# Keeping the experts' split weights in DRAM, starting the shared tiles inside the last sequence, and a wider last matrix product

## The chip, the cores and the metric

One core of one Trainium2 chip runs one kernel. The metric is device time in microseconds, the median of the runs, lower is better. All arithmetic is float32; TensorE takes its operands as fp32r.

## The reference, cut to what matters

```python
x = x + attention(layernorm(x))      # x: (8, 256, 256), 16 heads of 128, rotary positions, causal
x = x + ffn(layernorm(x))

def ffn(hidden):                     # 2048 rows of 256, 8 experts, inner width 176, top 2
    x = hidden.reshape(-1, H)
    topk_w, topk_idx = top_k(softmax(x @ gate_w.T), 2); topk_w /= sum(topk_w)
    y_all = einsum(silu(x @ w1[e]) * (x @ w3[e]), w2[e])      # per expert e
    shared = silu(x @ sw1) * (x @ sw3) @ sw2                  # inner width 352
    return sum of the two chosen y_all, weighted, + shared
```

## The kernel before, in words

Each engine has its own instruction list, written out by hand, and engines meet at semaphores. Nothing is planned at run time but the list of expert tiles.

**Split operands.** A float32 matrix product is made of three fp32r products (`three`, L546 to L552): every operand is held as a high part, a rounding copy by ScalarE (ACT), and a low part, the rest, by VectorE (DVE) or GpSimd (POOL). The weights are split too. A weight piece is loaded by SyncE (SP) into one of five slots of the tile `stage`, ACT writes the high part into the tile `w_hi` (`split_hi`, L1236 to L1241), and DVE (L868) or POOL (L1496) writes the low part into `w_lo` (`split_lo`). `w_hi` and `w_lo` have room for the attention's weights only; the weights of the second half (shared and experts', 30 pieces, pieces 32 to 61) go to the same places once the last sequence has read what was there.

**Attention.** Eight sequences (`sequence(b)`), each of 16 heads; FIRST is 0 and LAST is 7. In one head TensorE (PE) transposes the probabilities (L590), makes the scores of head h+2, projects q and k of head h+4, makes half a unit of values (512 columns wide), attends and adds the output of head h-1. ACT copies the high parts and does the exponentials, DVE masks, rotates (L894, L901) and takes low parts, POOL adds the two halves of the rotation (L446) and takes the low part of q and k (L1432). From sequence 1 on, the router's work for the sequence before is spread over the heads, and POOL scatters its rows to a DRAM tensor ordered by expert (`rows_by_expert`) with indirect DMAs at heads 12 to 15. That tensor is cleared first by nine DMAs of 2 MB (`clear`), after the last attention piece has been loaded. The transposed rows go to DRAM as well (`rows_transposed`) and come back as tiles of 128 rows in four slots (`rows_in`).

**The last sequence.** In its heads 0 to 14, 25 of the 30 pieces of the second half are split, two to a head at first, in turns by DVE and POOL. From head 11 on no rotation, projection or score is left to do. In heads 14 and 15 PE makes the two up-products of shared tile 0 (`up_s`).

**Shared tiles.** There are 16 (NT), of 128 rows: two up-products, Silu on ACT, product on DVE, transposition, high and low part, down-product, addition to `resid`. Tiles 0 to 7 (S1 = 8) stand ahead of the experts. Between them lie the router's work for the last sequence, the last five pieces (10 instructions on POOL), and the plan of the expert tiles on DVE (`plan_tiles`, L1093 to L1116).

**Experts.** 39 tiles (NJ) of 128 rows, each of one expert, which is read from a register. Steps on PE for tile j: transpose the rows (`turn_x`, L753), six up-products of 352 columns (`up_e`), transpose the activations (`turn_e`, L768), and the down-product (`down_e`):

```python
for k, r in ((0, P), (1, E_TAIL)):      # 128 and 48 rows of the inner width 176
    mm = three(p_yy[j % 2], [act_e[b][0:r, j % 2, k, :] for b in range(2)],
               [downs_e[b][0:r, bass.ds(e, 1), k, :] for b in range(2)], k == 0, k == 1)
```

ACT copies the result (L1349) and POOL scatters it to `results_by_token`.

**The end.** Shared tiles 8 to 15, and for each tile the two expert results, read back by SP (`result_in`) and added with their weights by DVE (`finish`, L1124 and L1128). SP waits for all experts' results to land before it issues `result_in` and the rows of tiles 12 to 15.

Of the kernel before, what the change touches and what calls it, by code (L numbers as in the profile page):

```python
# [7 lines left out]
F32 = mybir.dt.float32  # L8
F32R = mybir.dt.float32r
# [34 lines left out]
S1 = 8  # L44
XSLOTS = 4
ESLOTS = 8
RP = 7

# [4 lines left out]
def build(nc, x, wq, wk, wv, wo, gate_w, w1, w3, w2, sw1, sw3, sw2, cos_t, sin_t, mask_t, ident_t,  # L53
          order_t, base_t, own_t, route_t, plan_t, zero_t, out):
    ctx = ExitStack()
    with ctx:
# [59 lines left out]
        def wos(b):  # L116
# [11 lines left out]
        ups = [t[:, 0:NU * DC * UW].rearrange("p (u c m) -> p u c m", u=NU, c=DC) for t in whl]  # L128
        d0 = NU * DC * UW
        d1 = d0 + SB * D  # L130
        downs_s = [t[:, d0:d1].rearrange("p (n d) -> p n d", n=SB) for t in whl]
        downs_e = [t[:, d1:d1 + E * 2 * D].rearrange("p (e k d) -> p e k d", e=E, k=2) for t in whl]
        assert d1 + E * 2 * D <= G * GE

        back = [whl[t // S1][:, G * GE:].bitcast(F32)[:, t % S1 * TOP * D:(t % S1 + 1) * TOP * D] for t in range(NT)]
# [5 lines left out]
        wanted = route[:, 2 * E * E:].rearrange("p (c e) -> p c e", c=TOP)  # L141
        xs_slot = [t.rearrange("p (c s) -> p c s", c=DC)
                   for t in (cosn[:, :], sinn[:, :], work[:, 0:DC * P], work[:, DC * P:2 * DC * P])]
        xs_t = [t[:, :].rearrange("p (a c s) -> p a c s", a=2, c=DC) for t in xnt_all]
        sil_s = work[:, 512:512 + 2 * SI].rearrange("p (a m) -> p a m", a=2)
        acts_s = work[:, 512 + 2 * SI:512 + 4 * SI].rearrange("p (a m) -> p a m", a=2)
        act_s = [[t[:, 0:SB * P].rearrange("p (k m) -> p k m", k=SB) for t in two] for two in vbuf]
        e0 = 512 + 4 * SI
        sil_e = work[:, e0:e0 + 2 * I].rearrange("p (a m) -> p a m", a=2)
        acts_e = work[:, e0 + 2 * I:e0 + 2 * I + 4 * P].rearrange("p (a m) -> p a m", a=2)  # L150
        assert e0 + 2 * I + 4 * P <= 2816
        stage_all = stage[:, :, :].rearrange("p a b -> p (a b)")
        assert ESLOTS * RW <= NSTAGE * CH
        x_slot = [stage_all[:, n * RW:(n + 1) * RW] for n in range(ESLOTS)]
        y_slot = [v_late[n // 2][:, n % 2 * D:(n % 2 + 1) * D] for n in range(XSLOTS)]
        twin = [t[:, 0:RW] for t in v_late]
        xe_t = [t[:, :, :].rearrange("p a (c s) -> p a c s", c=DC) for t in qkt[0]]
        act_e = [t[:, :, :].rearrange("p a (k s) -> p a k s", k=2) for t in qkt[1]]
# [9 lines left out]
        room = work[:, e0:2816]  # L168
# [8 lines left out]
        assert e0 + o + 3 * NJ <= 2816  # L177
# [3 lines left out]
        res_d = nc.dram_tensor("results_by_token", (PAIRS + E * (S + P), D), F32, kind="Internal").ap()  # L181
        xt_d = nc.dram_tensor("rows_transposed", (B, P, ST * D), F32, kind="Internal").ap()
# [15 lines left out]
        p_turn = [cut(3, P), cut(0, P)]  # L198
        p_gate = [bank[a][:, 0:ST * E].rearrange("p (t e) -> p t e", t=ST) for a in (4, 1)]
        p_rank = [bank[a][:, 0:ST * E] for a in (3, 0)]  # L200
        p_total = [bank[a][:, ST * E:ST * E + E] for a in (3, 0)]

        p_us = [bank[2], bank[3]]
        p_as = [cut(4, P), cut(5, P)]
        p_yy = [bank[6][:, 0:D], bank[7][:, 0:D]]
        p_ue = [bank[0], bank[1]]
        p_xe = [cut(2, P), cut(3, P)]
        p_ae = [cut(4, P), cut(5, P)]
# [14 lines left out]
        w_lo = [sem("w_lo_dve"), sem("w_lo_pool")]  # L223

# [89 lines left out]

        REST = 57

        def lo_by(n):

            if n >= REST:
                return 1  # L320
            return int(n in (1, 3, 5, 6, 8, 11) if n < EARLY + 2 else n % 2 == 0)
# [60 lines left out]
        for u in range(NU):  # L382
            for c in range(DC):
                rc = slice(c * P, (c + 1) * P)
                if u < 2:
                    loads = [(lambda t: t[:, 0:UW], (sw1, sw3)[u][rc])]
                else:
                    loads = [(lambda t: t[:, 0:I], w1[u - 2][rc]), (lambda t: t[:, I:UW], w3[u - 2][rc])]
                add_piece(loads, [(lambda t: t[:, 0:UW], ups[0][:, u, c], ups[1][:, u, c])])
        for n in range(0, SB, 2):  # L390
            loads, seen = [], []
            for k in range(min(2, SB - n)):
                r = min(P, SI - (n + k) * P)
                view = lambda t, r=r, k=k: t[0:r, k * D:(k + 1) * D]
                loads.append((view, sw2[(n + k) * P:(n + k) * P + r, :]))
                seen.append((view, downs_s[0][0:r, n + k], downs_s[1][0:r, n + k]))
            add_piece(loads, seen)
        SHARED = len(pieces)
        for e in range(E):
            loads, seen = [], []  # L400
            for k, r in ((0, P), (1, E_TAIL)):
                view = lambda t, r=r, k=k: t[0:r, k * D:(k + 1) * D]
                loads.append((view, w2[e][k * P:k * P + r, :]))
                seen.append((view, downs_e[0][0:r, e, k], downs_e[1][0:r, e, k]))
            add_piece(loads, seen)
        NP = len(pieces)

        staged_count, total = [], [0] * NSTAGE
        for n, (loads, _) in enumerate(pieces):
            total[n % NSTAGE] += 16 * len(loads)  # L410
            staged_count.append(total[n % NSTAGE])

        def split_schedule():


            first = {0: 3, 1: 2, 2: 3} | {h: 2 for h in range(3, 9)}
# [34 lines left out]
        def _(sp):  # L451
# [19 lines left out]
            for n, (loads, _) in enumerate(pieces):  # L471
                if n == plan["last", 13][0] + NSTAGE:
                    sp.wait_ge(rope_mul, B * N)
                    for t in range(ST):
                        rows_in(t)
# [1181 lines left out]
```

## Time and profile before

| | |
|---|---|
| median of 3 runs | 792.18 us (790.72 to 793.57) |
| the profiled execution, its own time | 791.99 us |
| its span in the trace | 790.2 us |
| busy share: PE, DVE, ACT, POOL | 94%, 81%, 67%, 62% |
| chain that ended last, by engine | PE 74%, DVE 12%, ACT 4%, POOL 4% |
| granted TensorE clock, mean | 0.984 |

The profile gives each engine's busy time, and the share of the span in which the chain that ended last ran over it. Busy time of PE is modelled: what its stretches cost is read from the distances between the starts of its instructions. The shares are means over stages that have different limits, so the prediction reads it stage by stage.

### The profile page before, as it was taken

How to read it: one execution, taken by the hardware profiler on the slowest of the kernel's cores; microseconds unless marked ns; L12 is line 12 of the kernel's file. 1: busy time of each engine (PE TensorE's matmuls, PEld its weight loads, DVE VectorE, ACT ScalarE, POOL GpSimd, SP SyncE). 2: the span in 40 equal slices, each digit the busy share in tenths (PEclk: the TensorE clock that was granted, in tenths of full speed). 3: DMA queues.
4: the chain of work that ended last, by engine and by line, in shares of the span. 5: the costliest groups of instructions: out<-in, count | busy, mean ns of one | idle time of the engine just before them, and what ended most of it. 6: DMA issues, size and time to landing. Idle time of an engine off the chain costs nothing.

```text
span 790.2 us, 16279 instructions
## 1 busy us (share of the span) xinstructions
PE 742.8 (94%) x5520; PEld 698.5 (88%) x5520; DVE 640.2 (81%) x1766; ACT 532.0 (67%) x1667; POOL 486.9 (62%) x511
## 2 busy tenths in 40 slices
PE   5899999999999999999999999999996869999994
PEld 4788999999999999999999999998985868888883
DVE  6898889989898998999899989989994574444457
ACT  5788767767777777777777777677886425555531
POOL 5778566676767677766866776677785252333300
PEclk9999999999999999999999999999999979999998
DMA  6543434343000000000000000001323113333373
GB/s 202 152 154 105 178 160 188 148 188 149 14 8 21 15 1 15 14 15 2 27 2 14 8 22 15 1 21 44 89 74 86 46 61 94 108 108 107 101 259 101
DMA packets 36329, 61.59 MB, mean 78 GB/s; under 512 B 6808, under 2 KB 28280, under 8 KB 35672
## 3 DMA queue, kind: packets, MB, share of 16 engines
q1 hardware_dynamic: 32200, 49.14, 18.8%
q0 software_dynamic: 4048, 11.42, 4.0%
q8 instruction: 45, 0.74, 0.4%
q14 instruction: 36, 0.29, 0.1%
HBM read 47.03 MB, written 32.46 MB: 101 GB/s over the span
## 4 chain that ended last, share of the span: by engine, by line
PE 74%; DVE 12%; ACT 4%; POOL 4%; issue 2%; DMA 2%; SPq 0%; DVEq 0%; POOLq 0%
PE bank L550 59%; PE bank L590 4%; PE bank L583 3%; PE bank L599 3%; DVE work L901 3%; PE bank L753 2%; POOL work L446 2%; DVE work L894 1%; DVE w_lo L868 1%; PE bank L768 1%; ACT work L1257 1%; POOL qkt_lo L1432 1%; DVE pt_lo L922 1%; ACT w_hi L1240 1%; DVE work L910 1%
## 5 line engine op out<-in xcount | busy, mean ns | idle before, releaser
L1432 POOL TENSOR_TENSOR qkt_lo<-work,qkt_hi 128x512 fp32r<-128x512 f32 x128 | 166.5, 1301 | 80.6 <-ACT qkt_hi L1250 80.6
L446 POOL TENSOR_TENSOR work<-work 128x512 f32<-128x512 f32 x127 | 165.3, 1302 | 70.6 <-DVE work L901 64.2
L901 DVE TENSOR_TENSOR work<-bank,sinn 64x512 f32<-64x512 f32 x256 | 176.2, 688 | 3.4
L550 PE MATMUL bank<-xnt_hi,w_lo 128*128 128x256 f32 x512 | 146.1, 285 | 1.6 <-DVE xnt_lo L932 1.6
L550 PE MATMUL bank<-xnt_hi,w_hi 128*128 128x256 f32 x512 | 145.9, 285 | 0.0
L550 PE MATMUL bank<-xnt_lo,w_hi 128*128 128x256 f32 x512 | 145.8, 285 | 0.0
L1250 ACT CAST qkt_hi<-work 128x512 fp32r<-128x512 f32 x128 | 79.5, 621 | 93.2 <-POOL work L446 90.5
L1257 ACT ACTIVATE work<-work,bias 128x128 f32<-128x128 f32 (+1 forms) x256 | 112.7, 441 | 0.0
L894 DVE TENSOR_TENSOR work<-bank,cosn 128x512 f32<-128x512 f32 x128 | 87.9, 686 | 20.7 <-PE bank L550 20.6
L550 PEld LDWEIGHTS bank<-xnt_hi,w_lo 128*128 128x128 f32 x512 | 98.8, 193 | 2.2 <-DVE xnt_lo L932 2.2
L550 PEld LDWEIGHTS bank<-xnt_hi,w_hi 128*128 128x128 f32 x512 | 99.2, 194 | 0.0
L550 PEld LDWEIGHTS bank<-xnt_lo,w_hi 128*128 128x128 f32 x512 | 99.2, 194 | 0.0
L550 PE MATMUL bank<-w_hi,att_lo 128*128 128x256 f32 x256 | 82.9, 324 | 0.2 <-DVE att_lo L927 0.2
L1558 POOL DMA_INDIRECT results_by_token<-v_late,stage x39 | 37.5, 962 | 72.0 <-ACT v_late L1349 72.0
L910 DVE CUSTOM_DVE_ANT_0 work<-bank,mask 128x128 f32<-128x128 f32 (+1 forms) x256 | 78.5, 343 | 1.3 <-PE bank L550 1.3
L550 PE MATMUL bank<-w_hi,xnt_lo 128*128 128x512 f32 (+1 forms) x192 | 72.9, 380 | 7.0 <-DVE xnt_lo L1053 5.9
L550 PE MATMUL bank<-w_lo,att_hi 128*128 128x256 f32 x256 | 72.3, 282 | 0.0
L550 PE MATMUL bank<-w_hi,att_hi 128*128 128x256 f32 x256 | 72.1, 282 | 0.0
L550 PE MATMUL bank<-w_hi,xnt_hi 128*128 128x512 f32 (+1 forms) x192 | 72.0, 375 | 0.0
L550 PE MATMUL bank<-w_lo,xnt_hi 128*128 128x512 f32 (+1 forms) x192 | 71.3, 372 | 0.0
L927 DVE TENSOR_TENSOR att_lo<-bank,att_hi 128x256 fp32r<-128x256 f32 x128 | 54.1, 422 | 17.6 <-ACT att_hi L1290 14.7
L590 PE MATMUL bank<-ident,work 128*128 128x128 f32 x384 | 63.1, 272 | 0.7 <-ACT work L1263 0.6
(151 smaller groups left out, 2175.5 us busy)
## 6 DMA issues: line engine op xcount, KB each, us to landing
rows_by_expert<-in_zero_t SPq DMA_DIRECT2D x8, 2056.0 KB
stage<-rows_by_expert SPq DMA_DIRECT2D x39, 128.5 KB
stage<-in_L_ffn_w SPq DMA_DIRECT2D x32, 88.0 KB, 2.0
rows_by_expert<-in_zero_t SPq DMA_DIRECT2D x2, 1028.0 KB
resid<-in_L_attn_x SPq DMA_DIRECT2D x8, 256.0 KB, 3.7
stage<-in_L_attn_wv SPq DMA_DIRECT2D x8, 256.0 KB, 3.7
stage<-in_L_attn_wo SPq DMA_DIRECT2D x8, 256.0 KB, 2.8
rows_transposed<-xt POOLq DMA_DIRECT2D x8, 256.0 KB, 2.4
```

The lines of the kernel that those rows point to most:

```text
L446: eng.tensor_tensor(roped[:, a], rope_cos[:, a], rope_sin[:, a], ALU.add).then_inc(rope_add, 1)
L550: mm = pe.matmul(out, lhs[a], rhs[b], start=start and n == 0, stop=stop and n == 2, skip_group_check=more)
L583: pe.matmul(p_s[a][:, 0, 0:P], roped[:, a, 0, 0:P], roped[:, a, 1, 0:P], start=True, stop=True)
L590: mm = pe.transpose(p_t[:, k, :], prob[h % 2][:, k * P:(k + 1) * P], ident[:, :])
L894: nc.vector.tensor_tensor(rope_cos[:, a], p_qk[a][:, :, :], c, ALU.mult)
L901: op = nc.vector.tensor_tensor(rope_sin[lo:lo + 64, a], p_qk[a][hi:hi + 64, :, :], sn, ALU.mult)
L910: nc.vector.tensor_tensor_reduce(prob[a][:, cols], p_s[a][:, t, keys], mask[:, m], -SCALE, BIG, ALU.add, ALU.min, bias[:, a, t:t + 1]).the ...
L927: nc.vector.tensor_tensor(att[a][1][:, :], p_o[:, a, :], att[a][0][:, :], ALU.subtract).then_inc(o_lo, 1)
L1250: nc.scalar.copy(qkt[a][0][:, :, :], roped[:, a]).then_inc(qkt_hi, 1)
L1257: nc.scalar.activation(prob[a][:, c], prob[a][:, c], ACT.Exp, bias=bias[:, a, t:t + 1], scale=-1.0, accum_out=rsum[:, a, t:t + 1]).then_in ...
L1432: nc.gpsimd.tensor_tensor(qkt[a][1][:, :, :], roped[:, a], qkt[a][0][:, :, :], ALU.subtract).then_inc(qkt_lo, 1)
L1558: nc.gpsimd.indirect_dma_start(out=res_d, out_offset=bass.IndirectOffsetOnAxis(ap=x_slot[j % ESLOTS][:, D:RW].bitcast(I32), axis=0), in_=y ...
```

## The change

Three things, and what they need:

1. The 30 pieces of the second half are split in sequences 1 to 6, five to a sequence (heads 0, 2, 4, 8, 10), all low parts by POOL. Raw data use slot 0 of `stage`, the parts slots 1 to 4, and SP stores the parts in a DRAM tensor `w_d` (`add_kept`, `keep`). In the last sequence they are read back into `w_hi` and `w_lo` in large parts as groups of heads are done (`free`, `part_in`). The clears are cut in halves and issued between the pieces.
2. Shared tiles 0, 1 and the first half of 2 are worked in heads 12 to 15 of the last sequence; S1 is 9, so 7 tiles are left for the end. Silu writes to `acts_s` itself. The last sequence's rows lie in a tile `late`.
3. The experts' last matrix lies in `w_hi` alone, with its high and low part side by side (512 columns). The low part of the activations' second block stands in partitions 64 to 111 of the high tile. `down_e` has three products instead of six; their two halves are added by ACT (`half`) and DVE (`result`).

At the end, `finish` is called for two tiles in each of three steps instead of one in each of five. The diff, cut to its core:

```diff
-S1 = 8
+S1 = 9
...
+        def add_kept(loads, width, places):
+            pair = len(kept_at) % 2
+            parts = [stage[:, RAW + 2 * pair + b, :].bitcast(F32R)[:, 0:width] for b in range(2)]
+            add_piece(loads, [(lambda t: t[:, 0:width], parts[0], parts[1])])
+            kept_at.append([(stage[0:r, RAW + 2 * pair + b, at:at + n], w_d[a, q:q + r, to:to + n])
+                            for b, at, n, r, a, q, to in places])
...
+        for e in range(E):
             for c in range(DC):
...
+                add_kept([(lambda t: t[:, 0:I], w1[e][rc]), (lambda t: t[:, I:UW], w3[e][rc])], UW,
+                         [(b, 0, UW, P, 1, 0, e * UE + (b * DC + c) * UW) for b in range(2)])
+            loads, places = [], []
             for k, r in ((0, P), (1, E_TAIL)):
+                loads.append((lambda t, r=r, k=k: t[0:r, k * D:(k + 1) * D], w2[e][k * P:k * P + r, :]))
+                places += [(b, k * D, D, r, 0, 0, d0 + e * DE + (2 * k + b) * D) for b in range(2)]
+            places.append((0, D, D, E_TAIL, 0, 64, d0 + e * DE + 2 * D))
+            add_kept(loads, 2 * D, places)
...
+            heads += [(b, h) for b in range(1, LAST) for h in (0, 2, 4, 8, 10)]
...
+            for k in range(NK):
+                keep(k)
+                if k + 1 < NK:
+                    piece_in(NATT + k + 1)
+                if k % 5 >= 2 and parts_left:
+                    clear(*parts_left.pop(0))
...
+            for g in range(G):
+                free(g)
+                if g == G - 1:
+                    sp.wait_ge(rope_mul, B * N)
+                    rows_in(1)
+                    rows_in(2)
+                if g == 0:
+                    part_in(0, 0, d0, ups_in)
+                else:
+                    lo = max(0, 3 * g - 3)
+                    part_in(0, d0 + lo * DE, d0 + min(3 * g, E) * DE, experts_in)
+                part_in(1, 2 * g * UE, (2 * g + 2) * UE, experts_in)
+                if g == 0:
+                    rows_in(0)
...
-                    if b is LAST and h >= 14:
-                        up_s(0, h - 14)
+                    if b is LAST:
+                        if h == 12:
+                            up_s(0, 0)
+                        if h == 13:
+                            up_s(0, 1)
+                            up_s(1, 0)
+                        if h == 14:
+                            turn_s(0)
+                            up_s(1, 1)
+                        if h == 15:
+                            up_s(2, 0)
+                            turn_s(1)
...
             turn_s(S1 - 1)
             down_s(S1 - 2)
+            turn_x(0)
             down_s(S1 - 1)
...
-                for k, r in ((0, P), (1, E_TAIL)):
-                    mm = three(p_yy[j % 2], [act_e[b][0:r, j % 2, k, :] for b in range(2)],
-                               [downs_e[b][0:r, bass.ds(e, 1), k, :] for b in range(2)], k == 0, k == 1)
-                mm.then_inc(ye_ps, 1)
+                a = j % 2
+                pe.matmul(p_yy[a][:, :], act_e[0][:, a, 0, :], downs_e[:, bass.ds(e, 1), 0, :], start=True, stop=False)
+                pe.matmul(p_yy[a][:, 0:D], act_e[1][:, a, 0, :], downs_e[:, bass.ds(e, 1), 0, 0:D], start=False, stop=False)
+                pe.matmul(p_yy[a][:, :], act_e[0][0:64 + E_TAIL, a, 1, :], downs_e[0:64 + E_TAIL, bass.ds(e, 1), 1, :],
+                          start=False, stop=True).then_inc(ye_ps, 1)
...
+                nc.vector.tensor_tensor(act_e[1][:, a, 0, :], p_as[a][:, 0, :], act_e[0][:, a, 0, :], ALU.subtract)
+                nc.vector.tensor_tensor(act_e[0][64:64 + E_TAIL, a, 1, :], p_as[a][0:E_TAIL, 1, :],
+                                        act_e[0][0:E_TAIL, a, 1, :], ALU.subtract).then_inc(ae_lo, 1)
+
+            def result(j):
+
+                dve.wait_ge(half_done, j + 1)
+                nc.vector.tensor_tensor(y_slot[j % XSLOTS], y_slot[j % XSLOTS], p_yy[j % 2][:, 0:D], ALU.add).then_inc(ye_cp, 1)
...
+                        if h == 11:
+                            rows_high(0)
+                        if h == 12:
+                            silu_s(0)
+                            rows_high(1)
                         if h == 13:
-                            for t in range(ST):
-                                rows_high(t)
+                            rows_high(2)
+                        if h == 14:
+                            silu_s(1)
+                            high_s(0)
                         if h == 15:
-                            silu_s(0)
+                            silu_s(2)
+                            rows_high(3)
+                            high_s(1)
...
+                nc.scalar.copy(y_slot[j % XSLOTS], p_yy[j % 2][:, D:2 * D]).then_inc(half_done, 1)
...
-            for n in plan["rest"]:
-                split_lo(n)
             for j in range(NJ):
                 results_out(j)
```

## Rows read from the trace of the kernel before

**Rows 1.** Busy time by stretch: length, engines, granted clock, DMA share, GB/s.

```profile
535.00:592.93 57.93, 55.25 (x427) 51.68 (x425) 55.15 (x148) 48.05 (x151) 45.83 (x47) 1.00 0.25 71
592.93:612.90 19.97, 13.54 (x86) 11.61 (x84) 7.77 (x27) 12.61 (x41) 11.35 (x16) 0.91 0.33 89
652.67:743.40 90.73, 90.72 (x593) 80.31 (x593) 42.07 (x113) 48.87 (x149) 33.67 (x35) 1.00 0.36 108
764.00:767.00 3.00, 3.00 (x20) 2.99 (x19) 2.02 (x6) 0.84 (x3) 0.00 (x0) 0.78 1.05 395
779.20:790.19 10.99, 0.00 (x0) 0.00 (x0) 8.73 (x22) 0.00 (x0) 0.00 (x0) 0.64 0.43 144
```

**Rows 2.** Timeline of PE, first instruction of a head: sequences 6 and 7, heads 0 and 12.

```profile
463.17 0.49 PE L590 MATMUL bank<-ident,work 128*128 128x128 f32 x3
...
517.68 0.49 PE L590 MATMUL bank<-ident,work 128*128 128x128 f32 x3
...
535.00 0.49 PE L590 MATMUL bank<-ident,work 128*128 128x128 f32 x3
...
592.93 0.49 PE L590 MATMUL bank<-ident,work 128*128 128x128 f32 x3
```

**Rows 3.** Waits between 200 and 530 us: waiting engine and line, releaser, sum, times, longest.

```profile
POOL work L446 <- DVE work L901: 38.5, 51, 1.5
ACT pt_late L1274 <- PE bank L590: 19.3, 45, 0.7
```

**Rows 4.** Groups by form, POOL, 540 to 650 us: busy, mean ns.

```profile
L1496 POOL TENSOR_TENSOR w_lo<-stage,w_hi 128x352 fp32r<-128x352 f32 x10 | 9.4, 945 | 0.0
```

**Rows 5.** DMA issues of the whole run: KB each, median us to landing.

```profile
stage<-in_L_ffn_w SPq DMA_DIRECT2D x32, 88.0 KB, 2.0
```

**Rows 6.** Timeline of SP: it issues the two loads of one piece.

```profile
600.07 0.80 SPq L480 DMA_DIRECT2D stage<-in_L_ffn_w  x2
```

**Rows 7.** Timeline of POOL in sequence 1, head 14.

```profile
169.90 0.20 POOL L1543 TENSOR_SCALAR xn<-own 128x2 int32<-128x2 f32 x1 [1.85 <-DMA rows_by_expert<-xn,slot]
```

**Rows 8.** Timeline of ACT at the end of the last sequence.

```profile
611.57 1.28 ACT L1325 ACT_TABLE_LOAD   x1
```

**Rows 9.** Timeline of DVE and of POOL ahead of the experts.

```profile
637.85 5.72 DVE L1103 TENSOR_TENSOR work<-work,mask 128x64 f32<-128x64 f32 x1
...
637.27 6.89 POOL L1496 TENSOR_TENSOR w_lo<-stage,w_hi 128x256 fp32r<-128x256 f32 x10
```

**Rows 10.** Timeline of PE in one expert tile: its down-product, up to the next tile's start.

```profile
698.15 0.36 PE L550 MATMUL bank<-w_hi,qkt_lo 128*128 x1
698.35 0.28 PE L550 MATMUL bank<-w_hi,qkt_hi 128*128 x1
698.47 0.29 PE L550 MATMUL bank<-w_lo,qkt_hi 128*128 x1
698.68 0.38 PE L550 MATMUL bank<-w_hi,qkt_lo 48*128 x1
...
699.02 0.27 PE L550 MATMUL bank<-w_lo,qkt_hi 48*128 x1
699.23 0.44 PE L753 MATMUL bank<-ident,stage 128*128 128x128 f32 x2
```

**Rows 11.** Timeline of PE: products of 96 rows, and of 512 columns.

```profile
755.27 0.28 PE L550 MATMUL bank<-w_hi,v_lo 96*128 96x256 f32 x1
755.39 0.28 PE L550 MATMUL bank<-w_hi,v_hi 96*128 96x256 f32 x1
...
411.21 0.40 PE L550 MATMUL bank<-w_hi,xnt_lo 128*128 128x512 f32 x1
...
411.45 0.40 PE L550 MATMUL bank<-w_hi,xnt_hi 128*128 128x512 f32 x1
```

**Rows 12.** Chain that ended last, behind the last expert tile: start, us, what.

```profile
756.11 3.87 DMA cosn<-rows_transposed
...
760.91 3.11 PE bank L550 x12
```

More of the change, by code:

```diff
@@ L223, in build @@
         w_lo = [sem("w_lo_dve"), sem("w_lo_pool")]
+        blank = sem("blank")
+        kept = [sem(f"kept{a}") for a in range(2)]
+        ups_in = sem("ups_in")
+        downs_in = sem("downs_in")
+        half_done = sem("half_done")
+        experts_in = sem("experts_in")
         stats_done = sem("stats_done")
@@ L411, in build @@
-            staged_count.append(total[n % NSTAGE])
+            total[slot_of(n)] += 16 * len(loads)
+            staged_count.append(total[slot_of(n)])
+        FIRST, LAST = 0, B - 1
         def split_schedule():
-            first = {0: 3, 1: 2, 2: 3} | {h: 2 for h in range(3, 9)}
-            last = {h: 2 for h in range(11)} | {11: 1, 13: 1, 14: 1}
-            plan, n = {}, EARLY
-            for h in range(N):
-                plan["first", h] = list(range(n, n + first.get(h, 0)))
-                n += first.get(h, 0)
@@ L422, in split_schedule @@
[L422 to L427 removed]
+            heads = [(FIRST, h) for h, k in enumerate([3, 2, 3] + [2] * 6) for _ in range(k)]
+            heads += [(b, h) for b in range(1, LAST) for h in (0, 2, 4, 8, 10)]
+            assert len(heads) == NP - EARLY
+            plan = {}
+            for n, where in enumerate(heads, EARLY):
+                plan.setdefault(where, []).append(n)
@@ L432, in split_now @@
         def split_now(b, h):
-            which = "first" if b is FIRST else "last" if b is LAST else None
-            return plan.get((which, h), [])
-        FIRST, LAST = 0, B - 1
+            return plan.get((b, h), [])
         def wait(eng, s, value):
@@ new lines, in keep @@
+            def keep(k):
+                sp.wait_ge(w_lo[1], lo_count(NATT + k + 1, 1))
+                for part, there in kept_at[k]:
+                    sp.dma_start(there, part).then_inc(kept[k % 2], 16)
+            parts_left = [(k, half) for k in range(B + 1) for half in range(2)]
+            NK = NP - NATT
+            clear(*parts_left.pop(0))
+            clear(*parts_left.pop(0))
+            piece_in(NATT)
+            for k in range(NK):
[3 more added lines that the diff above has]
+                if k % 5 >= 2 and parts_left:
+                    clear(*parts_left.pop(0))
@@ new lines, in _ @@
+            sp.wait_ge(blank, 48)
+            for a in range(2):
+                sp.wait_ge(kept[a], kept_count(NK - 2 + (NK + a) % 2))
+            for g in range(G):
[12 more added lines that the diff above has]
+                    rows_in(0)
@@ L1214, in _ @@
             low_e(NJ - 1)
+            result(NJ - 2)
             for t in range(S1 + 1, NT):
@@ L1402, in _ @@
                 if j >= 2:
-                    result(j - 2)
+                    half(j - 2)
                 if j == 2:
@@ L1409, in _ @@
             high_e(NJ - 1)
-            result(NJ - 2)
+            half(NJ - 2)
             for t in range(S1 + 1, NT):
```

376 lines of the change are left out of this document (205 added, 171 removed).

## The prediction

> **What bounds the kernel now.** I read the stretches first [rows 1], then the starts of PE's heads [rows 2], the waits of the middle [rows 3], the timelines of the last sequence and of one expert tile, and the chain that ended last. The reader is to see four kinds of stage. In sequences 1 to 6 PE never pauses: a sequence takes 71.83 us (463.17 to 535.00 in [rows 2]), and ACT and POOL wait for others. In the last sequence heads 0 to 11 take 57.93 us where those of sequence 6 take 54.51 [rows 2]. From its head 12 on every engine is idle much of the time: PE is busy for 13.54 of 19.97 us, at a mean granted clock of 0.91 [rows 1]. The experts' tiles are PE's alone again: 90.72 of 90.73 us busy, with DVE at 42.07 and ACT at 48.87 [rows 1]. At the end PE waits once for rows from DRAM [rows 12], and DVE works 11 us alone [rows 1].
>
> **The split in sequences 1 to 6: 0 us taken, -1 to +6 kept.** Each of the 30 pieces adds one copy on ACT and one subtraction on POOL, 0.945 us for 352 columns [rows 4], a third more for the 512 columns of each third piece. Per sequence that is about 5 us on POOL. What hides it: ahead of its rotation sum POOL waits 38.5 us in 330 us [rows 3], 8.4 us per sequence, in portions of some 0.75 us; a piece of 0.945 us overlaps its portion or overruns it by 0.2. ACT waits 19.3 us there for the transposes [rows 3], 4.2 us per sequence, against five copies of about 0.5 us. DVE, the busiest of the three, gets nothing. What is late if the cover is gone: the high and low parts of q and k, so PE's scores. From above: the last sequence had 25 pieces, 23 of them in heads 0 to 10, on ACT and in turns on DVE and POOL, and lost 57.93 - 54.51 = 3.4 us [rows 2], 0.15 us a piece; 30 such pieces make 4.5 us. A load must also land in time, for ACT's copy stands in order ahead of the next head. Two heads are 2 x 54.51/12 = 9.1 us. POOL takes its part one head after ACT (4.5 + 0.95 us); SP then issues two stores and two loads at 0.4 us each [rows 6], and the load lands in 2.0 us [rows 5]: 9.1 us, just in time. After a piece of the last matrix there are five stores, 1.2 us more; five of those ten have only two heads to the next, and ACT's wait of 0.43 us a head [rows 3] takes a third: up to 4 us in all. The clears, in halves, run beside it. In sequence 1 POOL waited 1.85 us for a scatter that ran against a clear [rows 7]; a half is over before head 13, so this wait may go, a gain of up to 1 us. I take the two as 0, and -1 to +6 as bounds.
>
> **Reading the parts back: 0 us.** 12.2 MB come back in four lots of about 3 MB, the first three issued four heads (18 us) apart. The DMA engines moved 395 GB/s where they were full [rows 1], which makes 8 us for a lot. Queued behind the last lot, issued at head 12, are the rows of tile 3, which ACT needs at head 15, and the shared down weights, needed after it, some 13 and 18 us later. At half that rate they would be 3 us late, which is in the range.
>
> **Heads 0 to 11 of the last sequence: -3.4 us.** No split is left in them; 54.51 us as in sequence 6.
>
> **Heads 12 to 15: -2.2 us (+1 to -5).** ACT's 12.61 us [rows 1] lose three pairs of copies (2.1 us) and gain two Silus (0.9), one more copy of rows (0.4) and two high parts (1.1). They also gain table loads. Before there was one switch, from Exp to Silu, 1.28 us [rows 8]. Now Silu of tile 0 stands between the Exps of heads 14 and 15: Silu, Exp, Silu are three loads, 2.6 us more. That is 15.5 us of ACT in a row; with 1.5 us of waits for PE and DVE and the last output product (0.8) the heads take 17.8 instead of 19.97. PE has about 14.4 us of work in them, with five up-products instead of two, so ACT sets the pace, and the PE clock should stay up. The Trainium skill (ScalarE: Activation LUTs, What ACT_TABLE_LOAD costs) says a switch is a load of 1283 ns and a drain of 1380 ns. The row shows the load, with the copy before it ending 0.04 us earlier and the Silu right behind it; by the page the two further switches would cost 2.8 us more.
>
> **Shared tiles ahead of the experts: -1.9 and -5.5 us.** The same seven steps of a loop follow, but the first has one up-product instead of two and no wait for its Silu: the third step begins 7.0 us after the sequence instead of 8.9. Then the stall: one DVE product of 64 columns took 5.72 us [rows 9], and beside it POOL ran ten subtractions for 6.89 us. Other such small products take 0.2 to 0.3. These ten are gone, so the plan, and with it the first load of expert rows, comes 5.5 us sooner. The last down-product now covers the turn of tile 0. PE still idles for 3 to 4 us there, perhaps at the lower clock afterwards, so I count no more than the 5.5 (4 to 7).
>
> **The experts' down-product: -15.6 us (-5 to -17).** From start to start the six products take 699.23 - 698.15 = 1.08 us [rows 10]: 0.20, 0.12, 0.21 for the 128 rows, then 0.34 for two and 0.21 for the third of 48 rows. Products of 96 rows follow each other at 0.12 [rows 11], as those of 128 do; so 48 rows cost about 0.1 more on either side of a change and on the change back, 0.28 in all. Those of 512 columns stand 0.24 apart [rows 11]. The new three are 512, 256 and 512 columns, the last of 112 rows: 0.20 + 0.12 for the longer first, 0.12, and 0.24 if 112 rows behave as 96: 0.68. Saved 0.40 x 39 tiles = 15.6 us. If 112 rows pay as 48 do, 0.28 more: 0.12 x 39 = 4.7. Nearest to 112 is 96, so I take the first. The tile falls from 2.45 us (37 of them in 90.73) to 2.05. Then DVE, at 42.07/37 = 1.14 us a tile, gets a second subtraction and the addition of the halves, some 0.6 more: 1.75. ACT stays at 1.32, POOL with its scatter at 0.91. So PE still bounds, and the longer way of a result (0.4 us) is hidden by two tiles of lead.
>
> The Trainium skill (TensorE: Matmul & The Clock Gate, LDWEIGHTS) says that a weight load costs by its columns, and that 32 rows take as long as 128. By that the 48 rows cost nothing extra and the three shorter groups save 4.7 us (rival 1). The rows show the extra at 48, so I go by them.
>
> **The end: -4.6 us.** One shared tile fewer is left behind the experts, 3.3 us of PE. The wait for rows behind the last result stays: they took 3.87 us behind the issue and PE began at 760.91 [rows 12]; the way to them is 0.4 us longer by the addition of the halves, and two shorter down-products give 0.8 back. DVE works 8.73 us in 22 instructions after PE's end [rows 1], 0.4 each; two tiles fewer remain (1.6 us), but it starts 0.3 to 0.5 later, since `finish` now fills its steps to PE's pace. -0.4 - 3.3 - 0.9.
>
> **Sum.** 0 - 3.4 - 2.2 - 1.9 - 5.5 - 15.6 - 4.6 = -33.2 us. The profiled execution took 791.99 us for a span of 790.2; it is 0.2 below the median of the runs. 791.99 - 33.2 = **758.8 us**.
>
> **Rivals.**
> 1. *The down-product saves little* (16%). 112 rows pay as 48 do (0.96 a tile, above), or the gaps at 48 rows have another cause, which stays: at 0.12 for each product, the old six would be 0.80 against 0.68. Either saves 0.12 a tile, 4.7 us: 769.7. For it: no row shows 112. Against: the 96. The Trainium skill's rule on weight loads, above, is the second of these.
> 2. *Another engine bounds the expert loop* (11%). DVE's chain of five operations, or the ring from result to next load, holds the tile at 2.25: 7.8 us saved, 766.6. For it: DVE would be busy for 86% of a tile. Against: every hand-over has a tile of slack.
> 3. *The six sequences stretch* (16%) by 0.2 to 0.3 us a piece, since loads land late behind five stores: +8, 766.8.
> 4. *A table switch costs ACT twice its load* (6%), 2 x 1.28 us: 761.4. For it: in the row ACT had nothing in flight. By the Trainium skill's drain it is about this. Against: no gap behind the load.
> 5. *Slower* (4%). Every piece arrives late at ACT, in all 30 heads; it decides from 33/30 = 1.1 us a piece beyond ACT's slack of 0.4. At 1.4 us it costs 42, nine more than the gain: 801. My account has the usual piece just in time, so this needs SP or the stores to take 1.5 us more than [rows 5, 6] show.
> 6. *Little change* (2%): the same at 1.1 us a piece, 792.
> My forecast: 45%, 753 to 764.
>
> **Numbers.** From 751 to 772 holds the forecast and rivals 1 to 4. Faster than before by over 0.3% (2.4 us, about what this measurement can tell): 0.93; within: 0.02; slower: 0.05.
>
> **What the profile after would show.** Sequences 1 to 6: starts of heads 0 about 71.8 us apart, no wait of PE for q and k's low parts and none of ACT for `stage`. Last sequence: heads 0 to 12 in 54 to 55 us; three table loads; heads 12 to 15 in 17 to 18. Ahead of the experts: the product of 64 columns at 0.2 to 0.3 us. Experts: a tile in 2.05 us, the down-product's starts 0.32, 0.12 and 0.24 apart, PE without pauses. End: some 9 us from the last down-product to PE's restart, then three tiles. The prediction is wrong if the tile stays over 2.2, if PE's heads in sequences 1 to 6 are over 4.6 us apart on average, or if ACT waits for rows in heads 12 to 15.

## The result: 1.0% slower, where 4% faster was forecast

| | before | after |
|---|---|---|
| median | 793.57 us (790.72 to 794.12, 5 runs) | 800.9 us (798.97 to 802.89, 5 runs) |
| span of the profiled execution | 790.2 us | 799.1 us |
| granted TensorE clock, mean | 0.984 | 0.968 |

The ratio is 1.0101, with a 95% interval from 1.0072 to 1.013. The forecast was 758.8 us, 751 to 772, with a chance of 5% for slower. Both the number and the sign were wrong.

The stretches of the changed kernel show where. Six sequences, heads 0 to 11 and heads 12 to 15 of the last one, the stretch up to the first up-product of the experts, the experts up to the last turn of rows, the wait for rows, and the end; below them two short stretches that are used further on. Each line has the stretch, its length, the busy time of PE, PEld (PE's weight loads), DVE, ACT and POOL with the number of instructions, PE's granted clock, the busy share of the DMA engines, and what they moved in GB/s, all transfers together:

```profile
102.82:183.12 80.30, 74.50 (x566) 71.53 (x565) 65.86 (x188) 55.34 (x178) 55.85 (x59) 0.96 0.25 86
183.12:262.72 79.60, 73.85 (x567) 70.86 (x565) 65.02 (x186) 55.30 (x176) 55.04 (x58) 0.96 0.24 82
262.72:343.48 80.76, 74.81 (x567) 71.51 (x566) 65.88 (x188) 55.25 (x176) 56.16 (x59) 0.96 0.25 86
343.48:422.75 79.27, 73.90 (x567) 71.09 (x566) 65.13 (x186) 55.49 (x176) 55.16 (x58) 0.96 0.24 84
422.75:501.31 78.56, 73.95 (x567) 70.86 (x566) 65.42 (x187) 55.51 (x176) 55.78 (x58) 0.98 0.24 80
501.31:573.28 71.97, 71.97 (x566) 69.16 (x565) 65.25 (x187) 54.03 (x173) 54.79 (x57) 1.00 0.22 71
573.28:627.37 54.09, 54.09 (x427) 52.14 (x426) 48.47 (x138) 40.51 (x133) 35.87 (x37) 1.00 0.46 175
627.37:648.74 21.37, 16.71 (x110) 15.50 (x109) 8.98 (x30) 15.16 (x41) 7.44 (x10) 0.92 0.65 217
648.74:682.38 33.64, 28.79 (x203) 27.55 (x201) 20.40 (x67) 10.06 (x30) 8.43 (x18) 0.92 0.18 54
682.38:757.73 75.35, 74.82 (x471) 69.15 (x472) 57.42 (x178) 44.75 (x144) 32.33 (x34) 0.97 0.41 122
757.73:775.10 17.37, 16.06 (x108) 15.37 (x106) 10.40 (x33) 8.25 (x25) 5.20 (x6) 1.00 0.35 115
775.10:799.09 23.99, 13.10 (x93) 12.50 (x93) 20.02 (x54) 4.39 (x15) 0.00 (x0) 0.87 0.67 237
...
404.00:409.00 5.00, 5.00 (x42) 4.87 (x42) 4.47 (x15) 3.92 (x12) 3.61 (x4) 1.00 0.31 108
410.96:422.75 11.79, 6.42 (x37) 6.05 (x36) 3.74 (x11) 3.75 (x12) 6.11 (x7) 0.71 0.14 57
```

Sequence 6 takes 71.97 us, as before. Sequences 1 to 5 take 6.7 to 8.9 us more each. Everything from the last sequence on is 29.4 us shorter than before, where it took 255.2 (535.00 to 790.19, [rows 1, 2]). So the loss and the gain lie in different stretches and can be read apart.

One head holds the loss of a sequence. In sequence 4 head 15 starts at 410.96 and the next head at 422.75; a head in the middle takes 4.33 us. PE's timeline there:

```profile
410.96 0.49 PE L663 MATMUL bank<-ident,work 128*128 128x128 f32 x3
416.83 0.80 PE L656 MATMUL bank<-work 128*128 128x128 f32 x2 [5.37 <-POOL qkt_lo L1581]
...
418.06 0.41 PE L623 MATMUL bank<-xnt_hi,w_lo 128*128 128x256 f32 x1
418.27 0.41 PE L623 MATMUL bank<-xnt_hi,w_hi 128*128 128x256 f32 x1
```

PE waits 5.37 us for a low part of POOL, and afterwards its products stand 0.21 us apart instead of 0.12 for a while, at the lower of the two levels of its clock (1.2 instead of 2.4 GHz): over the stretch the mean granted clock is 0.71. The head is 7.46 us above one of 4.33: 5.4 are the wait, and the 2.1 that are left go with the lower clock, since no further wait stands in that stretch. POOL's timeline in the same place, and SP's:

```profile
406.20 0.99 POOL L1700 DMA_INDIRECT rows_by_expert<-xn,slot  x1 [0.16 <-issue]
...
415.36 0.19 POOL L1692 TENSOR_SCALAR xn<-own 128x2 int32<-128x2 f32 x1 [6.83 <-DMA rows_by_expert<-xn,slot]
415.51 1.26 POOL L1581 TENSOR_TENSOR qkt_lo<-work,qkt_hi 128x512 fp32r<-128x512 f32 x1
...
390.79 0.64 SPq L493 DMA_DIRECT2D rows_by_expert<-in_zero_t  x1
...
398.20 1.90 SPq L533 DMA_DIRECT2D weights_split<-stage  x2
400.14 0.92 SPq L501 DMA_DIRECT2D stage<-in_L_ffn_w  x2
403.56 0.64 SPq L493 DMA_DIRECT2D rows_by_expert<-in_zero_t  x1
```

At head 14 POOL must write the second index of the rows (L1692, `second_place`), and for that it waits until the scatters of heads 12 and 13 have landed. The one of head 13, issued at 406.20, lands 9.07 us later by the chain that ended last; in sequences 1 to 5 it takes 7.9 to 9.5. In the run with the clears moved, further on, the median of these scatters is 2.6. SP had issued a half clear at 403.56, which had itself waited for the half of 390.79 to land. Behind the waiting instruction stands q and k's low part. [Rows 7] showed the same wait at the same instruction, 1.85 us, once. Over the whole run, of the view of waits:

```profile
POOL xn L1692 <- DMA rows_by_expert<-xn,slot: 40.5, 7, 7.2
PEld bank L656 <- POOL qkt_lo L1581: 34.0, 10, 6.2
PE bank L656 <- POOL qkt_lo L1581: 31.0, 8, 5.9
```

Of the 40.5 us, 33.6 belong to sequences 1 to 5 and 0.2 to sequence 6. The seventh wait stands in the last sequence, where no clear is left:

```profile
640.18 0.19 POOL L1692 TENSOR_SCALAR xn<-own 128x2 int32<-128x2 f32 x1 [6.61 <-DMA rows_by_expert<-xn,slot]
```

There the DMA engines are busy reading the parts back. The same wait is 5.4 to 6.4 us in those runs of the changed kernel below that have their clears elsewhere or cut otherwise, and 2.2 in the kernel before, which reads nothing back. So it goes with the reading back and not with the clears, though no run changed the reading back alone. No low part of q and k is left behind it in POOL's list.

### The profile page after: what moved, and what is told of

The parts are those of the page before. It is cut to its first block, busy times and chain, and to the rows that moved or that the text cites. A ratio compares the mean times of both kernels' runs of the same rounds, so it can differ in the third digit from the quotient of the medians.

```text
span 799.1 us, 16176 instructions
## 1 busy us (share of the span) xinstructions
PE 733.4 (92%) x5403; PEld 695.8 (87%) x5403; DVE 645.8 (81%) x1831; ACT 531.2 (66%) x1661; POOL 493.3 (62%) x512
## 4 chain that ended last, share of the span: by engine, by line
PE 53%; DVE 16%; POOL 12%; DMA 9%; issue 5%; ACT 5%; SPq 1%; POOLq 0%; DVEq 0%
PE bank L623 40%; DMA rows_by_expert<-xn,slot 6%; DVE work L998 5%; POOL work L467 5%; POOL qkt_lo L1581 4%; PE bank L663 3%; PE bank L656 2%; DVE work L991 2%; PE bank L672 2%; DVE work L1007 1%; DMA results_by_token<-v_late,stage 1%; DVE pt_lo L1019 1%; PE bank L844 1%; DVE w_lo L965 1%; ACT work L1385 1%
## 5 line engine op out<-in xcount | busy, mean ns | idle before, releaser
L623 PE MATMUL bank<-xnt_hi,w_lo 128*128 128x256 f32 x512 | 149.0, 291 | 2.1 <-DVE xnt_lo L1029 2.1
L623 PE MATMUL bank<-xnt_lo,w_hi 128*128 128x256 f32 x512 | 148.4, 290 | 0.0
L623 PE MATMUL bank<-xnt_hi,w_hi 128*128 128x256 f32 x512 | 148.4, 290 | 0.0
L623 PEld LDWEIGHTS bank<-xnt_hi,w_lo 128*128 128x128 f32 x512 | 101.6, 198 | 3.0 <-DVE xnt_lo L1029 2.9
L623 PEld LDWEIGHTS bank<-xnt_hi,w_hi 128*128 128x128 f32 x512 | 102.0, 199 | 0.0
L623 PEld LDWEIGHTS bank<-xnt_lo,w_hi 128*128 128x128 f32 x512 | 101.9, 199 | 0.0
L623 PE MATMUL bank<-w_hi,xnt_hi 128*128 128x512 f32 (+1 forms) x256 | 82.7, 364 | 0.0
L656 PE MATMUL bank<-work 128*128 128x128 f32 x256 | 51.8, 285 | 31.2 <-POOL qkt_lo L1581 31.0
L1024 DVE TENSOR_TENSOR att_lo<-bank,att_hi 128x256 fp32r<-128x256 f32 x128 | 54.0, 422 | 18.5 <-ACT att_hi L1418 15.6
L656 PEld LDWEIGHTS bank<-work 128*128 128x128 f32 x256 | 39.3, 194 | 34.1 <-POOL qkt_lo L1581 34.0
```

Of the source, the lines that this page charges most:

```text
L623: mm = pe.matmul(out, lhs[a], rhs[b], start=start and n == 0, stop=stop and n == 2, skip_group_check=more)
L656: pe.matmul(p_s[a][:, 0, 0:P], roped[:, a, 0, 0:P], roped[:, a, 1, 0:P], start=True, stop=True)
L1024: nc.vector.tensor_tensor(att[a][1][:, :], p_o[:, a, :], att[a][0][:, :], ALU.subtract).then_inc(o_lo, 1)
```

## The experiments

The theory (A): the clears, not the splitting, cost the time. A scatter issued behind a half clear lands about when the clear does, and a half is as long as a whole clear was. The rivals: POOL's new subtractions or the pieces' stores and loads delay the sequences (B), and for the length of a half, that its bytes and not its shape set it (A2).

### The clears of the changed kernel issued behind the first three pieces of a sequence

```diff
-                if k % 5 >= 2 and parts_left:
+                if k % 5 <= 2 and parts_left:
```

> The changed kernel with its clears issued behind the first three pieces of a sequence instead of the last three; nothing else differs. Theory A (the scatter of head 13 lands only with a clear that SP issued 2.4 us before it, and POOL, then PE, wait for it): the last half of a sequence is under way from about head 5 and has landed before head 12, POOL waits under 1 us at head 14, a sequence takes 71.9 us, and the 38.3 us that sequences 1 to 5 lost come back: about 763 us. Theory B (POOL's splitting work or the stores and loads of the pieces delay the sequences): nothing comes back, 798 to 803. If both share the loss, in between.

Measured: 783.74 us, ratio to before 0.9887 [0.986, 0.9913]. POOL's wait at head 14 sums to 2.2 us over the six sequences, so that part of A held. But only 17 of the 38 us came back, between the two theories. The rest moved to heads 5 and 6 of a sequence: head 5 takes 6.9 to 10.7 us in sequences 1 to 5, where it took 5.2 before. The view of waits, and ACT's timeline at one such place:

```profile
ACT stage L1368 <- DMA stage<-in_L_ffn_w: 13.7, 8, 3.7
...
277.25 0.48 ACT L1368 CAST stage<-stage 128x352 fp32r<-128x352 f32 x1 [2.69 <-DMA stage<-in_L_ffn_w]
```

That is the piece of head 4. SP issues its load at 272.58, when the slot is free, and ACT wants it at 274.56, so it is needed just when an undisturbed load lands (2.0 us, [rows 5]). The half of 262.36 was still running. ACT's copy stands in order, so the next q and k wait with it.

### The halves cut by rows instead of by experts

```diff
-                rows, some = slice(k * S, min((k + 1) * S, REGION)), slice(half * E // 2, (half + 1) * E // 2)
-                here = xs_d[0:E * REGION, :].rearrange("(e r) d -> e r d", e=E)[some, rows, :]
+                size = (min((k + 1) * S, REGION) - k * S) // 2
+                rows = slice(k * S + half * size, k * S + (half + 1) * size)
+                here = xs_d[0:E * REGION, :].rearrange("(e r) d -> e r d", e=E)[:, rows, :]
```

> The changed kernel with every clear cut in halves by rows (all eight experts, half of the rows) instead of by experts (four experts, all rows); issued at the same places, with the same bytes. Theory A1 (a clear is spread over as many DMA engines as it has experts, so a half by experts takes as long as a whole one, 12.8 us from issue to landing): the half by rows lands in about 7 us, POOL waits 1 to 2.5 us at head 14 instead of 6.9, and PE 0 to 1.5: 763 to 772 us. Theory A2 (the bytes or the DRAM set the time of a clear, not the number of engines): the half still takes 12.8 us, 798 to 803.

Measured: 767.26 us, ratio 0.967 [0.963, 0.971]. The same bytes at the same places of the program, cut along the other axis, are worth 34 us. POOL still waits 0.7 to 2.7 us at head 14 in sequences 1 to 5. POOL in sequence 1, where the changed kernel had waited 6.89 us:

```profile
169.89 0.19 POOL L1693 TENSOR_SCALAR xn<-own 128x2 int32<-128x2 f32 x1 [1.54 <-DMA rows_by_expert<-xn,slot]
```

The length of a half is seen best where two are issued one after the other (from a later run with the same cut, behind the piece of head 4 of sequence 1): the two issues, the second of which waits for the first half to land, take 8.40 us, so the half took 7.7. In the changed kernel the two were 12.77 us apart (390.79 and 403.56). The rate while one runs, in that later run, counts everything that the DMA engines moved in the stretch:

```profile
132.62 8.40 SPq L494 DMA_DIRECT2D rows_by_expert<-in_zero_t  x2
...
134.00:139.00 5.00, 5.00 (x42) 4.87 (x41) 4.94 (x13) 3.27 (x12) 3.74 (x6) 1.00 0.54 213
```

213 GB/s at a share of 0.54, against 108 at 0.31 for a half by experts. A whole clear of the kernel before, over all eight experts, moved 206 at 0.48, and the clears there were issued 13.15 us apart on the mean. So A2 is out: half of the bytes at half of the rate is the same time. The Trainium skill (DMA: Bandwidth & Descriptors, Why a DMA increments its semaphore by 16 and not by 1) says that a transfer uses as many DMA engines, up to 16, as divide its slowest dimension evenly. For four and eight experts the rates and shares agree with that; how many engines a clear used is not shown by itself.

### The kernel before, with its clears alone changed

```diff
-                    for k in range(B + 1):
+                    for k in range(2 * (B + 1)):
+                        if k > 1:
+                            b = 1 + (k - 2) // 3
+                            sp.wait_ge(s_ps, b * N + (9, 12, 16)[(k - 2) % 3])
                         clear(k)
```

with `clear` cutting by experts as in the changed kernel.

> The kernel before with its clears alone changed: halves by experts, three to a sequence, the last one issued at head 13's scores, as in the changed kernel; no splitting in sequences 1 to 6, no stores. Theory A: POOL waits about 7 us at head 14 in sequences 1 to 5, they lose about 38 us less the 1.0 us that sequence 1 lost before: 829 to 832 us. Theory B (splitting and its stores are what costs): 791 to 796.

Measured: 821.96 us, ratio 1.0368 [1.035, 1.0386], against 829 to 832 expected. Without one instruction of the splitting the sequences lose the time. Sequence 2, sequence 5, and POOL in sequence 4:

```profile
184.37:263.16 78.79, 73.89 (x566) 71.08 (x565) 65.21 (x186) 53.52 (x171) 50.72 (x53) 0.96 0.13 51
...
420.34:493.66 73.32, 72.06 (x566) 69.26 (x565) 65.42 (x187) 51.92 (x168) 49.43 (x52) 1.00 0.12 48
...
413.24 0.19 POOL L1547 TENSOR_SCALAR xn<-own 128x2 int32<-128x2 f32 x1 [6.47 <-DMA rows_by_expert<-xn,slot]
```

The size was 7 to 10 us off. Sequences 1 to 4 lose 6.6 to 6.8 us each, against 7.4 to 8.9 in the changed kernel, and sequence 5 only 1.5. The half issued there is one of the last clear, which has 128 rows instead of 256, and POOL went on 7.8 us after its issue (480.25), against 11.5 in sequence 4 (401.69). In the changed kernel the same small half was issued 0.9 us ahead of head 13's scatter, and cost 6.7.

### Both: cut by rows, and early

> The changed kernel with clears both cut by rows and issued behind the first three pieces of a sequence. The run that moved them alone gained 17 us, not 38, and lost the rest at heads 5 and 6, where ACT waited up to 3.7 us for a load of the next piece. Theory A1 (everything that is issued behind a clear on its DMA engines lands with it, scatters and loads alike; a half by rows is over in 7 us): no scatter and at most short loads meet a clear, a sequence takes 71.9 to 72.5 us, 762 to 766 in all. Theory E (the early loads are late for another reason, the five stores or SP's issues): ACT still waits for the loads of head 4, sequences take 74 to 75, 778 to 784.

Measured: 763.67 us, ratio 0.9654 [0.9621, 0.9687]. ACT's waits for the pieces are 4.5 us in six sequences instead of 13.7 in the first run, and the gap at heads 5 and 6 is gone. So most of that lateness came from the clears and not from SP's five stores. What is left stays at 4.2 us in the next run, where the clears are elsewhere again; its cause was not looked for.

### Cut by rows, two behind the piece of head 4 and one behind that of head 8

```diff
-                if k % 5 >= 2 and parts_left:
-                    clear(*parts_left.pop(0))
+                for _ in range((0, 0, 2, 1, 0)[k % 5]):
+                    if parts_left:
+                        clear(*parts_left.pop(0))
```

> The changed kernel with clears cut by rows, two behind the piece of head 4 and one behind the piece of head 8, none behind that of head 10. By theory A1 all of them run where neither a load that is needed soon nor a scatter is issued: a sequence takes 71.9 us, POOL waits under 0.5 us at head 14, and 4 us more are won than with the halves by rows at the old places (767.3): 762 to 764 us. Rival: the second clear, which makes SP wait 7 us, delays the store and load of the piece of head 8, and 2 to 5 us are lost at its ACT copy.

Measured: 763.82 us, ratio 0.9647 [0.9619, 0.9675]; expected 762 to 764. The rival's delay did not come. The six sequences take 433.5 us (71.85 to 73.00 each), against 432.0 in the kernel before. So with the clears out of the way, splitting 30 pieces, storing them and loading them costs 1.5 us net. Against six sequences of 71.83 us it is 2.5, for before the change sequences 1 and 2 were 1.0 us longer than that.

### And one table load instead of three in heads 12 to 15

```diff
                         if h == 13:
                             up_s(0, 1)
-                            up_s(1, 0)
                         if h == 14:
+                            up_s(1, 0)
                             turn_s(0)
...
                         if h == 12:
-                            silu_s(0)
                             rows_high(1)
                         if h == 13:
+                            silu_s(0)
                             rows_high(2)
```

> The run before it, and the Silu of shared tile 0 moved behind the last Exp (head 13), the first up-product of tile 1 moved to head 14: one table load instead of three in heads 12 to 15. Theory F (heads 12 to 15 are one chain through ACT, in which the two extra loads stand): 1.5 to 2.6 us less than the run before it, heads 12 to 15 in 19 to 20 us instead of 21.4. Theory G (the chain there is that of attention heads, DVE and PE; table loads fill ACT's waits): within 0.5 us of it. Worse by up to 1 us, if the later Silu makes PE wait longer in head 14 than the loads cost.

Measured: 761.7 us, ratio 0.9614 [0.9583, 0.9644]. The medians differ by 2.1 us, with intervals that overlap, and the two profiled executions (763.82 and 764.13 us) do not differ as wholes: what this stage gained there, others lost. The profiles show the step in its stage. Heads 12 to 15 in the run before it and in this one, then the table loads of the changed kernel and of this one:

```profile
590.67:610.67 20.00, 15.12 (x110) 13.90 (x109) 8.98 (x30) 15.18 (x41) 7.44 (x10) 1.00 0.68 232
```

```profile
591.57:609.60 18.03, 14.84 (x110) 13.95 (x109) 8.99 (x30) 12.51 (x39) 7.57 (x10) 1.00 0.75 257
```

```profile
631.70 1.28 ACT L1467 ACT_TABLE_LOAD   x1
635.58 1.28 ACT L1385 ACT_TABLE_LOAD   x1
642.94 1.28 ACT L1467 ACT_TABLE_LOAD   x1
```

```profile
599.52 1.28 ACT L1469 ACT_TABLE_LOAD   x1
```

ACT is busy 2.67 us less, and the stage is 1.97 us shorter, within the 1.5 to 2.6 of theory F; its 19 to 20 us were counted from 21.4, and the run before it already had 20.00. The last run below has the same order of work and takes 18.02. So most of the two loads, 1.97 of 2.56 us, stood in the chain of the stage. The run also moved an up-product from head 13 to head 14, and what that gave or cost by itself was not tried.

### The clears with the rows as the outermost dimension

```diff
-                here = xs_d[0:E * REGION, :].rearrange("(e r) d -> e r d", e=E)[:, rows, :]
+                here = xs_d[0:E * REGION, :].rearrange("(e r) d -> r e d", e=E)[rows]
```

(and the source likewise), once on the run cut by rows and once on the last one.

> As the run with halves by rows at the changed kernel's places, but each clear is written with the rows as the outermost dimension (128 rows) and the experts inside, so in 1024 pieces of 1028 bytes instead of 32 of 32,896. The Trainium skill (DMA: Bandwidth & Descriptors, Why a DMA increments its semaphore by 16 and not by 1) says that a DMA runs on as many of the 16 engines as the slowest dimension allows. From the runs alone: a clear over four experts moved 108 GB/s and took 12.8 us, one over eight moved 213 and took 7.7. If the count of the outermost dimension sets the rate, this one takes 4 to 6 us, POOL waits at head 14 under 1 us a sequence, and the time is 763 to 765 instead of 767.3. If small pieces cost what the larger number of engines gives, or hold up the scatters more, it is 766 to 771.

> The run with one table load and moved clears, and its clears with the rows as the outermost dimension too. Only about 1.5 us over six sequences is left to win there, so by the first theory 760 to 762, the same as that run within its uncertainty; by the second 762 to 765.

Measured: 767.3 us, ratio 0.9696 [0.9663, 0.9729], and 762.67 us, ratio 0.963 [0.9603, 0.9657]. Nothing is gained. Two issues again take 8.41 us, and the rate in the same stretch as above (134 to 139 us) is hardly higher, though the share is:

```profile
132.72 8.41 SPq L494 DMA_DIRECT2D rows_by_expert<-in_zero_t  x2
...
134.00:139.00 5.00, 5.00 (x42) 4.87 (x41) 4.94 (x13) 3.27 (x13) 3.74 (x6) 1.00 0.92 220
```

So from four experts to eight the rate doubled, and with 128 rows outermost it rose from 213 to 220 GB/s, while the share of the DMA engines' time went from 0.54 to 0.92. Whether the small pieces eat the gain or copies inside DRAM have a limit of their own stays open; no run here tells the two apart.

### The kernel before, with 128 rows in place of 48 in the experts' second block

```diff
-                for k, r in ((0, P), (1, E_TAIL)):
+                for k, r in ((0, P), (1, P)):
                     mm = three(p_yy[j % 2], ...
```

> The kernel before with the second block of the experts' down-product taken over 128 rows instead of 48; the 80 further rows hold leftovers, so the experts' part of the output is not the reference's. The number of products stays at six. Theory C (a change between 128 and 48 rows costs about 0.1 us each way, which is where the larger part of the tile's gain in the changed kernel comes from): the starts inside the down-product stand 0.12 apart, the tile falls from 2.45 us to 2.11, and 39 tiles save 13 us: about 780. Theory D (48 rows cost nothing extra, the gaps have another cause): tile at 2.45, 791 to 795.

Measured: 777.26 us, ratio 0.9819 [0.979, 0.9847]. PE in one tile's down-product of this run, then in the changed kernel's:

```profile
701.94 0.36 PE L550 MATMUL bank<-w_hi,qkt_lo 128*128 x1
702.14 0.28 PE L550 MATMUL bank<-w_hi,qkt_hi 128*128 x1
702.26 0.28 PE L550 MATMUL bank<-w_lo,qkt_hi 128*128 x1
702.38 0.28 PE L550 MATMUL bank<-w_hi,qkt_lo 128*128 x1
702.50 0.28 PE L550 MATMUL bank<-w_hi,qkt_hi 128*128 x1
702.62 0.28 PE L550 MATMUL bank<-w_lo,qkt_hi 128*128 x1
702.73 0.39 PE L753 MATMUL bank<-ident,stage 128*128 128x128 f32 x2
```

```profile
706.25 0.48 PE L873 MATMUL bank<-w_hi,qkt_hi 128*128 x1
706.56 0.28 PE L874 MATMUL bank<-w_hi,qkt_lo 128*128 x1
706.68 0.40 PE L875 MATMUL bank<-w_hi,qkt_hi 112*128 x1
706.91 0.38 PE L844 MATMUL bank<-ident,stage 128*128 128x128 f32 x2
```

More rows, the same count of products, and the tile falls from 2.45 us to 2.12: 0.34 a tile, of which 0.29 lies in the down-product (1.08 to 0.79) and 0.05 in the transposition behind it, which also follows a change from 48 rows. The changed kernel's three products take 0.66 and its tile 1.98. So of the 0.47 us a tile that it saves, 0.34 come from not having 48 rows any more, and only 0.13 from three products in place of six. For 39 tiles the 0.34 makes 13.3 of the 15.1 us between the medians; the rest was not traced.

## Why the prediction was wrong, step by step

| step | predicted | measured |
|---|---|---|
| up to sequence 1 | 0 | -0.2 |
| sequences 1 to 6 | 0 (-1 to +6) | +38.5 |
| last sequence, heads 0 to 11 | -3.4 | -3.8 |
| heads 12 to 15 | -2.2 (+1 to -5) | +1.4 |
| up to the experts' first up-product | -1.9 - 5.5 = -7.4 | -6.1 |
| experts and end | -15.6 - 4.6 = -20.2 | -20.8 |
| sum | -33.2 | 9.0 (the spans: 8.9) |

**The step that failed** is one sentence of the first term: "a half is over before head 13, so this wait may go". It put this wait at nothing, and of the 38.5 us it made 37: 1.5 are left with the clears moved. It was wrong twice. It took half of the bytes for half of the time, and a half by experts takes 12.8 us, as a whole clear did. And it did not place the halves: even those cut by rows, 7.7 us long, left 0.7 to 2.7 us of the wait at the same places. The trace of before was nearly enough for that. A piece's stores begin two heads behind its head, so the first half of a sequence is issued at about 30 us; the second behind the stores of head 8's piece, at 46; the third must wait for it, 13 us, and runs from about 60 to 73. Head 13's scatter is issued at 63. The profile has 31, 47 and 60. The wait of 1.85 us in [rows 7] was the warning. That scatter had met the end of a clear once, by chance of the phase. The change gave each of five sequences a clear that starts just ahead of that scatter. I named the right wait and forecast its end where it grew to 33.6 us in sequences 1 to 5.

**The other costs of the split** were right at 0: 1.5 us over six sequences, once the clears are elsewhere. The fear that loads come late at ACT was right in its mechanism, and the first experiment shows it, but the thing in front of them is a clear and not the five stores. Rival 5, the only slower one, had every piece late at ACT. In the changed kernel ACT waits for pieces for 4.0 us in all, so that its 801 us stand next to the measured 800.9 is luck. Two signs that the prediction had named came: PE waits for q and k's low parts (31.0 us), and its heads in sequences 1 to 6 are 4.90 us apart on average, over the 4.6 at which it called itself wrong.

**The clock** had no place in the first term. Of 7.5 us lost in a gap, 2.1 go with the lower clock behind it.

**Heads 0 to 11**: right. **Heads 12 to 15**: mis-sized by 3.6 us. I added up ACT (15.5 us), 1.5 us of waits and 0.8 for the last product. ACT is busy 15.16 us, as said, but the stage took 21.37, so ACT stands idle for 6.2: it waits inside the chain, 2.31 and 1.49 us for PE alone. Part of it is the clock. Head 14 in the changed kernel, then in the run with moved clears:

```profile
636.63:643.25 6.62, 4.69 (x26) 4.45 (x25) 1.55 (x5) 3.69 (x13) 2.36 (x4) 0.74 0.78 279
```

```profile
599.93:605.00 5.07, 3.13 (x26) 2.90 (x25) 1.37 (x5) 3.53 (x13) 2.27 (x4) 1.00 0.97 319
```

PE stood idle for 1.93 us in the one and 1.94 in the other, yet only in the one the granted clock fell; why is open. All four heads took 20.00 us there, so about 1.4 of the 3.6 is the clock. With one load it took 18.03. Two loads of 1.28 us fewer gave 1.97 us, so rival 4, that a switch costs twice its load, did not happen.

**Ahead of the experts**: the product of 64 columns takes 0.21 us instead of 5.72, as said. The idle time of PE was 3.66 us at the end of it, within the 3 to 4 named. The first load of expert rows comes 7.6 us sooner in the stage, where the two terms had 7.4. But the first up-product follows the load after 5.6 us instead of 4.1, since the last shared down-product, 2.1 us at a granted clock of 0.50, now stands between the first transposition of rows and that up-product; before, it stood ahead of both. So only 6.1 us were gained.

**The down-product**: starts 0.31, 0.12 and 0.23 apart, where 0.32, 0.12 and 0.24 were forecast; 112 rows behave as 96. The tile takes 1.98 us, 0.07 less than forecast, mostly because the transposition behind it gets faster too. Over the 35 down-products between the first up-product and the last turn that makes 16.4 us; 12.9 were measured. About 2.4 of the difference lie at the start, where PE's granted clock was 0.50 up to 684.29 and 0.79 up to 691.01, behind the idle time (an estimate: 0.50 x 1.91 + 0.21 x 6.72). The rest is in three later tiles of 2.1 to 2.6 us, one of which waits 0.4 us for its rows. The prediction said that the clock might be lower at the start and counted nothing for it. Rivals 1 and 2 are out.

**The end**: the restart 17.37 us behind the last turn instead of 19.98, and the rest 23.99 instead of 29.28, as the sum had it.

So the terms behind the sequences were right to 3.9 us in 33, nearly all of it in heads 12 to 15. With the clears cut by rows and moved the kernel runs at 763.8 us, and with one table load at 761.7, the fastest here: 3.9% less than before, and 2.9 us above the forecast.

## What to carry to other kernels

When a change moves a background transfer, put each transfer on the time axis next to every small one that somebody waits for: start, length, and what the issuing queue waits for first. And do not take half of a transfer for half of its time: here a half that had four experts instead of eight in the outermost dimension took as long as the whole, and a half with all eight and fewer rows took 7.7 us instead of 12.8. Then look who stands behind the instruction that waits: here 6.8 us in which POOL waited to write an index cost PE 7.5, because the low part of q and k came next in POOL's list.

## What the runs showed of the hardware

- Scatters issued by POOL and loads issued by SP landed late when a clear issued earlier by SP was still under way: a scatter took up to 9.5 us, where the median in the run with the clears moved was 2.6, and ACT waited up to 3.7 us for a load. The Trainium skill (DMA: Bandwidth & Descriptors, Issuing engines are not separate DMA queues) says that DMAs of all issuing engines run on the same 16 engines; the trace agrees.
- While a copy inside DRAM over four experts ran, the DMA engines moved 108 GB/s, over eight 206 to 213, and with 128 rows outermost, in pieces of 1028 bytes, 220 (share of their time: 0.31, 0.48 to 0.54, 0.92).
- Three products of 48 rows among six cost 0.34 us a tile more than the same number of 128 rows, 0.05 of it in the transposition behind them, which had not been expected. With 112 rows the starts stood 0.12 and 0.23 us apart, as near as with 128 (0.12 and 0.24).
- The same idle time of PE (1.93 and 1.94 us, same place in the program) was followed by a mean granted clock of 0.74 in one run and 1.00 in another.
